# Attention and feed-forward kernel: the last two units' blocks by halves in two row tiles instead of in the whole array

## What is computed

```
h   = LN(x)
q, k, v = h Wq^T, h Wk^T, h Wv^T        16 heads of 16
y   = (softmax(q k^T / 4) v) Wo^T
x   = x + LN(y)
z   = LN(x);  zp = z shifted by one token (zero ahead of the batch)
r   = sigmoid((mu_r z + (1 - mu_r) zp) Wr^T)
k   = relu((mu_k z + (1 - mu_k) zp) Wk'^T) ** 2
out = x + LN(r * (k Wv'^T))
```

## Time and profile before

| what | value |
|---|---|
| median of three runs | 1295.94 us (1295.87 to 1299.86) |
| profiled execution, its own time | 1295.87 us |
| its span | 1294.1 us |
| its mean granted TensorE clock | 0.998 of full speed |
| ScalarE busy | 1065.4 us (82%) |
| VectorE busy | 786.1 us (61%) |
| GpSimd busy | 272.4 us (21%) |

### The profile page before, as it was taken

The page is one execution under the profiler, slowest core; times in us unless marked ns, Lnnn a source line. Parts: engine busy times, 40 slices in busy tenths (PEclk is TensorE's granted clock), DMA queues, the critical chain, the costliest instruction groups (busy, mean ns, idle before and its releaser), DMA issues.

```text
span 1294.1 us, 25293 instructions
## 1 busy us (share of the span) xinstructions
PE 1270.3 (98%) x10514; PEld 602.5 (47%) x10514; DVE 786.1 (61%) x1729; ACT 1065.4 (82%) x1149; POOL 272.4 (21%) x353
## 2 busy tenths in 40 slices
PE   8999999999999999999999999999999999999996
PEld 5544444444544444454444445444544544333344
DVE  6653746657474764857466574747647474544636
ACT  3688888888888888888888888888888888888851
POOL 1000212222211322122122222113222221222211
PEclk9999999999999999999999999999999999999999
DMA  4365563317712294215733176122832057301000
GB/s 151 101 143 172 99 132 76 94 50 136 127 42 75 72 167 90 65 52 105 137 78 91 51 141 121 44 74 77 169 83 60 26 106 138 68 1 33 1 17 16
DMA packets 61796, 112.68 MB, mean 87 GB/s; under 512 B 6512, under 2 KB 31344, under 8 KB 61616
## 3 DMA queue, kind: packets, MB, share of 16 engines
q1 hardware_dynamic: 61360, 109.60, 37.9%
q10 hardware_dynamic: 288, 1.05, 0.3%
HBM read 68.42 MB, written 41.94 MB: 85 GB/s over the span
## 4 chain that ended last, share of the span: by engine, by line
PE 89%; DVE 6%; ACT 3%; issue 1%; POOL 1%; DMA 0%; ACTq 0%
PE O L613 36%; PE S L594 25%; PE M L360 14%; PE M L347 10%; PE M L247 2%; ACT PT L601 2%; DVE sth L670 1%; DVE A L679 1%; PE M L497 1%; DMA A<-w_dram 0%; DVE xB L694 0%; POOL rsh L675 0%; DVE xnT L423 0%; DVE mvh L672 0%; PE S L1001 0%
## 5 line engine op out<-in xcount | busy, mean ns | idle before, releaser
L601 ACT ACTIVATE PT<-S 128x1024 f32<-128x1024 f32 x1024 | 1006.1, 1026 | 172.3 <-PE S L594 171.9
L613 PE MATMUL O<-PT,V 128*17 128x512 f32 x4096 | 538.9, 598 | 0.9 <-ACT PT L601 0.8
L594 PE MATMUL S<-QS,KS 50*128 50x512 f32 x2048 | 462.6, 453 | 4.6 <-ACT PT L601 4.6
L594 PEld LDWEIGHTS S<-QS,KS 50*128 50x128 f32 x2048 | 207.9, 183 | 460.4 <-ACT PT L601 351.2
L613 PEld LDWEIGHTS O<-PT,V 128*17 128x17 f32 x4096 | 67.8, 95 | 140.4 <-issue 135.4
L674 POOL TENSOR_SCALAR veh<-mvh 128x2 f32<-128x2 f32 x96 | 22.3, 232 | 503.5 <-DVE mvh L672 503.5
L813 DVE SCALAR_TENSOR_TENSOR A<-Z,M 128x512 f32<-128x512 f32 x30 | 20.5, 682 | 157.4 <-PE M L360 157.4
L347 PE MATMUL M<-xnT,WH 64*128 64x512 f32 x512 | 112.4, 395 | 3.2 <-DVE xnT L423 3.2
L360 PE MATMUL M<-WH,xnT 64*128 64x256 f32 (+1 forms) x504 | 83.1, 278 | 0.3 <-DVE xnT L423 0.3
L360 PE MATMUL M<-WH,B 64*128 64x256 f32 (+1 forms) x464 | 79.0, 280 | 1.0 <-DVE B L747 1.0
L360 PE MATMUL M<-WH,C 64*128 64x256 f32 (+1 forms) x464 | 78.9, 280 | 0.9 <-DVE C L777 0.9
(11 more groups left out here) (115 smaller groups left out, 1634.2 us busy)
## 6 DMA issues: line engine op xcount, KB each, us to landing
scr<-p SPq DMA_DIRECT2D x124, 256.0 KB
QS<-scr SPq DMA_DIRECT2D x56, 256.0 KB, 6.8
KS<-scr SPq DMA_DIRECT2D x56, 256.0 KB, 11.0
QS<-scr SPq DMA_DIRECT2D x70, 128.0 KB, 6.4
KS<-scr SPq DMA_DIRECT2D x68, 128.0 KB, 8.8
xA<-x_dram SPq DMA_DIRECT2D x16, 512.0 KB, 7.0
xB<-x_dram SPq DMA_DIRECT2D x16, 512.0 KB, 5.2
out_dram<-xB SPq DMA_DIRECT2D x15, 512.0 KB, 3.1
```

The source lines that it names most:

```text
L594: fn = lambda e, p=p, a=a, rows=rows: e.matmul(PS[p][:, a, :], KS[qd][rows, p, kt * 128:kt * 128 + 128], QS[qd][rows, p, hf * 512:hf * 512 ...
L601: e_fn = lambda e, p=p: e.activation(PT[i % 2][:, 2 * p:2 * p + 2, :], PS[p][:, :, :], ACT.Exp, scale=SCALE)
L613: fn = lambda e, j=j: e.matmul(PO[32 * j:32 * j + 17, :], V[b % 2][:, kt, 4 * qd + j, :], PT[i % 2][:, j, :], start=(kt == 0), stop=(kt == 7))
```

## The change

In all units blocks now go by halves in the two row tiles; the whole-array mode (solo) of units 14 and 15 is gone, and their age stays 2 up to s = 19 and 1 after. The tail's own blocks are as before.

```diff
@@ class Block
-                self.seen, self.queued, self.tokens, self.solo = None, queued, tokens, False
+                self.seen, self.queued, self.tokens = None, queued, tokens
@@ begin
-            block = None if solo[0] and now[0] is not None else choose(age)
+            block = choose(age)
             if isinstance(block, Turn):
                 turns.append(block)
                 return False
             now[:] = block, now[0]
-            if block is not None and now[1] is None and solo[0]:
-                block.solo = True
-                tile[0] = queue(block.half(PM[block.bank[0]], 2), *block.waits[0])
-                return True
             if now[0] is not None:
...
@@ step_part
             emit(*limit, ends)
-            if ends[0] is not None and now[0].solo:
-                block = now[0]
-                now[0] = None
-                until_rest(block.done(block.bank[0], PM[block.bank[0]], ends[0]))
-            elif ends[0] is not None:
+            if ends[0] is not None:
                 now[0].token = ends[0]
             if ends[1] is not None:
...
-        solo = [False]
@@ the loop over the steps
-                age, solo[0] = (2 if s < 20 else 1, True) if b + 1 == B else (1, False)
+                age = 2 if b + 1 == B and s < 20 else 1
                 pump(0 if u == 0 and s < 9 else 32 - s, age, (lambda: scores(i + 1, 1)) if nxt else None)
                 values(i)
```

## The result

| | before | changed |
|---|---|---|
| median of 20 executions each | 1297.83 us (1295.87 to 1301.52) | 1295.67 us (1291.42 to 1298.86) |
| profiled execution, its own time | 1295.87 us | 1293.49 us |
| its span | 1294.1 us | 1291.5 us |
| its mean granted TensorE clock | 0.998 | 0.995 |

The ratio is 0.9977, with a 95% interval of 0.9967 to 0.9988: 3.0 us less, between 1.6 and 4.3. That is a gain, but it lies within the 0.3% named in the prediction, and the median is outside the predicted range (1288.8 to 1294.2).

A forecast was written before the change was run, and what follows sets the result against it. TensorE, busy 98% of the span, was taken as the bound, so step length on it mattered. From 1295.87, the loop's -11.1, VectorE's order +5.2 and the clock +1.5 gave 1291.5 us, range 1288.8 to 1294.2.

The forecast's parts named there:

- Schedule: Steps 448 to 511: 40 steps with halves, and v1's second half, 12 matmuls, left over behind the last PV.
- Pace of 2.36 without charge for banks or VectorE: Attention loop: 39 steps with halves at 2.36 make 92.04, against 2.75 per whole-array step, no waits charged.
- rival 5: A bank or wait stalls the chain, or unit 14 ends otherwise: up to 3 us, 1294.5; chance 0.10.
- rival 4: Array form does not give the 0.39 per step, halves still cost 2.75: 1307; chance 0.03.
- Light steps: Loop steps without block work: two stretches of ten at 20.72 each, two single steps at 2.01 each.
- Behind the loop: After the last PV, VectorE's order delays y0 to 10.68 instead of 5.48: +5.2, bounds 3.7 and 6.
- Rival 2: VectorE's order hurts less or the last half is overtaken, y0 under 2 us late: 1286.8; chance 0.05.
- Clock: At y0 after 3.8 us idle, TensorE falls to 1.2 GHz: +1.5, bounds 0 and +2.9.
- Rival 1: Clock holds over the idle time before y0, or that time is short: 1290.0; chance 0.27.
- rival 3: Clock stays at 1.2 GHz through y0, y1 and the nine filler pairs: +10.3, 1300.3; chance 0.05.
- The base: Starting level for the total: 1295.87, the profiled execution, with the median of three at 1295.94.
- The gain of the median: Whole-kernel change from three terms: loop -11.1, tail order +5.2, clock +1.5, giving 1291.5 from 1295.87.

The follow-up runs named there:

- Unit 14 alone: Kernel before with halves in unit 14, whole-array blocks kept only in unit 15: 1295.09 us against 1299.81 for before, ratio 0.9959.
- nine fillers: Changed kernel with nine fillers instead of five ahead of y0: 1294.73 us against 1299.81 for the kernel before, ratio 0.9957.
- no fillers in the old kernel: Kernel before without its five fillers ahead of y0: 1302.20 us against 1297.92 with them, ratio 1.0023.
- third repeat: Changed kernel run again unaltered, a single execution: 1290.83 us against 1295.95 for one execution of the kernel before.
- two repeats: Changed kernel run again unaltered, twice: 1295.27 us against 1299.81 for before, and 1297.02 against 1299.34; ratios 0.9963 and 0.9978.
- second repeat: Changed kernel run again unaltered: 1297.02 us against 1299.34 for the kernel before, ratio 0.9978.
- first repeat: Changed kernel run again unaltered: 1295.27 us against 1299.81 for the kernel before, ratio 0.9963.
- the two profiles with the waits filled: Matmuls added into TensorE's waits at 29.4 and 35.7 us: kernel before 1298.30 us (ratio 0.9998), changed kernel 1292.44 (0.9957), both against 1297.92.
- the run with doubled steps: Changed kernel with steps 508 to 510 doubled so no block is left over: 1289.66 us against 1299.34 for the kernel before, ratio 0.9938.
- age 1: Changed kernel with age 1 throughout instead of 2 up to s = 19: 1292.60 us against 1297.92 for the kernel before, ratio 0.9954.

## Why the prediction was right or wrong

- **Schedule.** Right, step by step: 40 steps with halves, 12 matmuls left over, light stretches of ten steps at 458 and 490, two light ones at 482.
- **Pace of 2.36 without charge for banks or VectorE.** Right: 39 steps took 18.87 + 32.97 + 14.17 + 25.91 = 91.92, where 92.04 was forecast, so that rival 5, a stall of the chain, is out. Unit 14 alone shows both paces in one execution, which ends rival 4.
- **Light steps.** Mis-sized by 0.36: the two stretches took 20.54 each, not 20.72. With the two light steps at 3.95 and the last at 1.88, the loop gave -11.64, where the term was -11.1. By the bounds ("if the first is shorter, -0.5") it is covered.
- **Behind the loop.** Right, 10.63 against 10.68 worked out. L803 starts 2.69 after PV(511) (2.65 forecast), the first L669 1.61 after that (1.60), and the next links take 1.35, 1.37 and 3.61, where 1.35, 1.35 and 3.73 were taken from the earlier trace rows. Rival 2 is out.
- **Clock.** Right in kind, too small in most profiles: "I take the middle, +1.5". The three ways to read it say 2.2 to 2.4: y0 and y1 at 5.25 instead of 2.94, nine fillers take away 2.36, no fillers in the old kernel cost 2.2. There y0 starts inside the fall, and the clock comes back only when the y's are done. In the third repeat y0 starts at full clock at 1250.08, the clock is down from 1251.0 to about 1254.4 only, and the cost is 1.50; that this is the middle I had taken is luck, since I had no row for the way back. Rival 1 is out with that, and rival 3 too: nearly all of the nine filler pairs run at full clock.
- **The base.** This is the step that failed: "1295.87 (the profiled execution; the median of the three, 1295.94, is 0.07 above)". I took one execution, without an early fall, for the level of the median; the three runs, one of them at 1299.86, had already shown the other kind. The median of 20 is 1297.83, 1.96 higher. From there the same terms give 1293.4, and a range of the same width around it, 1290.8 to 1296.2, would have held the 1295.67.
- **The gain of the median.** It makes up the other half of the 4.2 by which the forecast was too low. Forecast -4.4, worked out from the profiles -4.1, measured -3.0 (1.6 to 4.3) by the ratio and -2.2 between the medians; in the two repeats the medians moved by 4.5 and 2.3. The terms of the loop and the tail are off by 0.3 together. Like against like they hold: the four lowest of the 20 executions, 1291.42 to 1291.88, stand at the 1291.7 that the sum gives with the loop and the tail as measured, 4.5 under the six lowest of before, and with the short fall in the tail the sum is 1290.9, beside the third repeat's 1290.83. What is left is the mix of executions with and without falls, which the sum has no term for, and which I can't work out.

**What stays open.** Executions of the changed kernel at 1297.0 to 1297.4 (seven of twelve in the second repeat) have no profile; the third repeat was meant to show one and caught a short one, 1290.83. Their distance to those without an early fall, about 6.3, would be 3.1 (fall at 37) + 0.85 (the longer fall in the tail) + 2.0 for a fall at 8 us. Such a fall was recorded in two kernels (below), and before's group at 1301 lies 1.9 above its group at 1299.5. Their mean clock is 0.992 or 0.993, where the executions at 1294.8 to 1295.9 beside them have 0.993; the rest is arithmetic, not a record. Whether the change makes long executions more frequent is open too: of the changed kernel 15 of 39 are at 1296.8 or more, of before 16 of 71 at 1300.7 or more, which is not clear of chance.

## What to carry to other kernels

Price a block by what stands on both sides of it: whole-array work between row-tiled scores cost 0.39 per step here, nearly all of it beyond the matmuls' own time, and was worth avoiding though the matmuls double in number. When a schedule grows longer by a step or two, look at what falls off its end, and there at the in-order engine behind it: here 5.15 of 11.64 came back by the order on VectorE and 2.35 by the clock, and two lines that issue the urgent work first won back 5.3. And take the base from many executions: a change of 4 us can't be placed absolutely on a kernel that has steps of 1.4 and 3 us between one execution and the next; compare executions of the same mean clock.

## What the runs showed of the hardware

- **The clock can fall behind short waits.** Ahead of the fall at 37 us TensorE had waited 0.89 at this score pair; the kernel before has the same wait at 36.66 and kept its clock, and so did the third repeat. Of the twelve profiles of kernels without matmuls added there, ten show the fall; the two profiles with the waits filled don't. What decides between them isn't shown. The first repeat, timeline of TensorE, at the point where its clock falls:

```profile
36.61 0.50 PE L584 MATMUL S<-QS,KS 50*128 50x512 f32 x2 [0.89 <-ACT PT L591]
```

  It then stayed at 1.2 GHz to about 43.7, under matmuls without a gap, which is 3.1 us lost; in the changed kernel's first profile the fall is half as long and costs 1.6. In the tail, where the wait was 3.5, y0 and y1 ran nearly all of their time at that level in three of the profiles, and a part of it in the third repeat (0.70 in 1252 to 1256). The Trainium skill ("TensorE: Matmul & The Clock Gate", Part 1) says that the number of slow matmuls at a kernel's start varies from run to run, which these runs bear out for a fall later on, and that "the ramp penalty is <1% of a typical kernel span". The early fall is 0.24% here (3.1 of 1298), as much as the effect that was to be measured.

- **A second early fall.** Unit 14 alone and the kernel before without fillers, neither of which touches the start, show the clock at 0.52 and 0.50 in 8 to 10 us. Unit 14 alone, TensorE's windows:

```profile
8.00:10.00 2.00, 1.97 (x9) 0.52 1.09 367
```

  With both falls its PV(449) is at 1105.76, 2.05 behind that of the second repeat, which has only the later one; in the kernel without fillers it is at 1106.63.

- **VectorE beside GpSimd.** In the run with doubled steps, VectorE's pair of L669 took 1.67 instead of 0.73 beside GpSimd's addition (1.26), and L627 took 0.69 instead of 0.43 beside the next one (1.27); the transposes kept their 0.70. With age 1, L627 beside that addition took 0.69 too. The work that was meant to be moved off VectorE cost it 1.2 there. That GpSimd is the cause is read from the overlap; no run changed it alone.
